# One-hots in twelve instructions with pointer scalars, and an add in four pieces, in a graph and mixture-of-experts kernel

## What is computed

```python
x = x + gnn0(layernorm(x))      # 2 graph convolutions, each a weighted sum over edges
x = x + moe0(layernorm(x))      # 6 experts, top 2 of each node
x = x + gnn1(layernorm(x))      # messages relu(mish(node)[src] + mish(edge)), summed over edges
x = x + moe1(layernorm(x))      # 8 experts, top 2

# one graph convolution of gnn0
msgs = support[edge_src] * edge_weight[:, None]
agg = jax.ops.segment_sum(msgs, edge_dst, num_segments=num_nodes)

# the message part of gnn1
y = mish(edge_features @ W_edge.T + b_edge)
msg = jax.nn.relu(x[src] + y)
agg = jax.ops.segment_sum(msg, dst, num_segments=node_features.shape[0])
```

## Time and profile before

| | |
|---|---|
| median of 3 runs | 5182.44 us |
| the profiled execution | 5180.41 us |
| its span | 5178.6 us |
| PE busy | 3895.7 us (75%) |
| POOL busy | 2875.4 us (56%) |
| DVE busy | 1965.5 us (38%) |
| ACT busy | 1566.8 us (30%) |
| mean granted TensorE clock | 0.731 |

### The profile page before, as it was taken

The page is one execution under the profiler, slowest core; times in us unless marked ns, Lnnn a source line. Parts: engine busy times, 40 slices in busy tenths (PEclk is TensorE's granted clock), DMA queues, the critical chain, the costliest instruction groups (busy, mean ns, idle before and its releaser), DMA issues. The chain is left out here.

```text
span 5178.6 us, 61257 instructions
## 1 busy us (share of the span) xinstructions
PE 3895.7 (75%) x16707; PEld 3012.1 (58%) x16707; DVE 1965.5 (38%) x4145; ACT 1566.8 (30%) x1876; POOL 2875.4 (56%) x2950
## 2 busy tenths in 40 slices
PE   3688888885788898896959966666666667769980
PEld 2455555553556565564548755666666665558870
DVE  4344344433344444433423354333333334511113
ACT  1344444443344444443201145212122123411110
POOL 0677777772777777772420055777777772600007
PEclk9778788876787778776579976555555556689995
DMA  3455555554454554552132234666666662242214
GB/s 95 140 175 171 166 173 173 177 169 116 125 156 150 157 157 150 155 156 69 66 130 85 81 113 133 197 200 197 201 199 199 200 198 61 82 154 65 65 61 144
DMA packets 336091, 733.21 MB, mean 142 GB/s; under 512 B 67797, under 2 KB 184672, under 8 KB 335897
## 3 DMA queue, kind: packets, MB, share of 16 engines
q1 hardware_dynamic: 160968, 392.16, 21.9%
q0 software_dynamic: 118176, 284.72, 20.1%
q10 hardware_dynamic: 56880, 55.58, 3.2%
HBM read 521.27 MB, written 210.91 MB: 141 GB/s over the span
## 5 line engine op out<-in xcount | busy, mean ns | idle before, releaser
L582 PE MATMUL conv_pz<-conv_we,conv_edge 128*128 128x256 f32 x3360 | 1221.0, 498 | 0.0
L1188 PE MATMUL x_pa<-x_hot,x_node 128*128 128x64 f32 x3360 | 765.7, 423 | 359.6 <-PEq L72 359.6
L464 POOL DMA_INDIRECT conv_gath<-support_table,conv_idx x840 | 808.0, 962 | 404.1 <-issue 249.8
L1173 POOL DMA_INDIRECT x_node<-node_table,x_idx x840 | 852.3, 1015 | 297.2 <-issue 234.9
L464 POOL DMA_INDIRECT conv_gath<-hidden_table,conv_idx x840 | 808.8, 963 | 346.7 <-issue 247.4
L1188 PEld LDWEIGHTS x_pa<-x_hot,x_node 128*128 128x128 f32 x3360 | 732.5, 331 | 393.0 <-issue 393.0
L582 PEld LDWEIGHTS conv_pz<-conv_we,conv_edge 128*128 128x128 f32 x3360 | 729.3, 241 | 181.7 <-issue 49.5
L573 PE MATMUL conv_ps<-conv_hot,conv_gath 128*128 128x64 f32 x3360 | 524.5, 311 | 358.9 <-DMA conv_gath<-support_table,conv_idx 187.7
L573 PEld LDWEIGHTS conv_ps<-conv_hot,conv_gath 128*128 128x128 f32 x3360 | 474.0, 221 | 404.5 <-DMA conv_gath<-support_table,conv_idx 197.3
L883 ACT ACTIVATE conv_q<-conv_q 128x1024 f32<-128x1024 f32 x210 | 221.9, 1057 | 1201.2 <-ACTq L72 1176.9
L1209 DVE TENSOR_TENSOR x_node<-x_node,x_neg 128x1024 f32<-128x1024 f32 x210 | 257.4, 1226 | 626.4 <-DMA x_node<-node_table,x_idx 626.4
(11 more groups left out here) (221 smaller groups left out, 4234.4 us busy)
## 6 DMA issues: line engine op xcount, KB each, us to landing
conv_edge<-in_edge_t SPq DMA_DIRECT2D x210, 512.0 KB, 5.0
edge_mish_table<-conv_neg SPq DMA_DIRECT2D x210, 512.0 KB, 3.1
x_neg<-edge_mish_table SPq DMA_DIRECT2D x210, 512.0 KB, 3.5
e_rows<-expert_rows SPq DMA_DIRECT2D x114, 256.0 KB, 3.0
expert_outs<-e_outs ACTq DMA_DIRECT2D x114, 256.0 KB, 2.2
expert_outs<-conv_zeros ACTq DMA_DIRECT2D x35, 512.0 KB
conv_gath<-support_table,conv_idx POOLq DMA_INDIRECT x840
conv_gath<-hidden_table,conv_idx POOLq DMA_INDIRECT x840
```

Of the source, the lines that this page charges most:

```text
L464: pool.indirect_dma_start(gath[s][:, j, :], None, table[:, :], bass.IndirectOffsetOnAxis(ap=idx[:, half, col:col + 1], axis=0),).then_inc( ...
L582: pe.matmul(ps_z[r][:, j, :], edge[r][:, m, j * P:(j + 1) * P], we[:, m, :], start=m == 0, stop=False)
L1173: pool.indirect_dma_start(node[s][:, j, :], None, c.t3[:, :], bass.IndirectOffsetOnAxis(ap=idx[:, half, col:col + 1], axis=0),).then_inc(g ...
L1188: last = pe.matmul(ps_a[n][:, m, :], node[s][:, j, m * P:(m + 1) * P], hot[n][:, j, :], start=j == 0, stop=j == CG - 1)
```

## The change

In `stage_conv`, `one_hots` first copies the half's 12 columns of `rel` and of the weights into a small tile `at_hot`, and then makes the 12 one-hots with one `tensor_scalar` each: its one tensor input is `iota` (64 columns), and its two scalars are pointers to a column of `at_hot`, compared with and multiplied by in the same instruction. In `stage_edges`, the add of `neg` to `node` is done chunk by chunk, in four instructions of 128x256; the semaphore that ScalarE waits for is raised by the last.

```diff
+        at_hot = [sb(f"at_hot{half}", [P, 2, HALF_COLS]) for half in range(2)]
...
             def one_hots(i, half):
-                part_of = lambda a: a[:, bass.ds(i * (SLOTS * CG) + half * HALF_COLS, HALF_COLS)].unsqueeze(2).to_broadcast([P, HALF_COLS, W])
-                link(dve, nc.vector.tensor_tensor(hot[half][:], c.iota[:].unsqueeze(1).to_broadcast([P, HALF_COLS, W]), part_of(rel), ALU.is_equal), own)
-                nc.vector.tensor_tensor(hot[half][:], hot[half][:], part_of(c.weight), ALU.mult).then_inc(hot_ready[half], 1)
+                part_of = lambda a: a[:, bass.ds(i * (SLOTS * CG) + half * HALF_COLS, HALF_COLS)]
+                nc.vector.tensor_copy(at_hot[half][:, 0, :], part_of(rel))
+                link(dve, nc.vector.tensor_copy(at_hot[half][:, 1, :], part_of(c.weight)), own)
+                for j in range(HALF_COLS):
+                    last = nc.vector.tensor_scalar(hot[half][:, j, :], c.iota[:], at_hot[half][:, 0, j:j + 1], at_hot[half][:, 1, j:j + 1],
+                                                   ALU.is_equal, ALU.mult)
+                last.then_inc(hot_ready[half], 1)
...
                 dve.wait_ge(gathered[s], k * (IT * CG * 16) + i * (CG * 16) + CG * 16)
-                nc.vector.tensor_tensor(node[s][:], node[s][:], neg[s % RING][:], ALU.add).then_inc(own, 1)
+                for j in range(CG):
+                    last = nc.vector.tensor_tensor(node[s][:, j, :], node[s][:, j, :], neg[s % RING][:, j, :], ALU.add)
+                last.then_inc(own, 1)
```

## The result

The changed kernel takes 5126.89 us (median of 4 runs, 5119.7 to 5141.69) against 5178.93 us of the kernel before, run in turn with it on the same chip: a ratio of 0.9903, interval 0.9881 to 0.9925. The prediction was 5141 us. The profiled execution is the slowest of the four, 5141.69 us with a span of 5139.9; against the profiled 5180.41 us of before it is 39 us shorter, not 52.

A forecast was written before the change was run, and what follows sets the result against it. POOL's gathers were taken to bound both aggregations and the edge stage. -28 - 16 + 3 = -41 us from 5180.4 gave 5139, and 5141 us for the median of runs; own range 5118 to 5163, overall 5112 to 5186.

The forecast's parts named there:

- 840 times (gather + gap): Both aggregations and edge stage: POOL never rests, so its gathers and 0.30 us gaps set each stage's length.
- Edge stage, -28 us: Edge stage: 58 us of gather excess removed, 20 and 10 us of waits returned by pieces and one-hots.
- term for the pieces: Edge stage: gathers that meet a piece of the add wait 0.095 us on average, 210 times: 20 us.
- term for the one-hots: Edge stage: the two-input one-hot instruction now comes closer before the next gather and delays some: 10 us.
- Rival 2: Edge stage: pieces don't help, saved waits return elsewhere; only the aggregations count: 5169 us, chance 0.21 with its no-change end.
- Aggregations, -16 us: Both aggregations: 31 us of gather excess removed, 15 us returned by the bursts of twelve tensor_scalar.
- rival 1: Aggregations: bursts of tensor_scalar cost POOL nothing, so -30 us there: 5127 us, chance 0.14.
- the danger: Aggregations: double-rate tensor_scalar may hold what POOL needs; 27 or 1 us by length of hold, 15 taken.
- Index waits, +3 us: Aggregations: VectorE's later adds bring the index copies nearer to POOL's need, costing 3 us.
- own sign of being wrong: POOL: index waits that add up to over 20 us would show the prediction wrong.
- Sum: Whole kernel: edge stage -28, aggregations -16 and index waits +3 make -41 us.
- Rival 3: Aggregations: POOL's second demand is many small grabs, each losing to a tensor_scalar; +56 us, 5238 us, chance 0.11.

The follow-up runs named there:

- f1: The changed kernel itself, both parts, run again against the kernel before (5184.49 us): 5138.83 us, ratio 0.9919.
- f2: The kernel before with only the edge stage's add in four pieces, against the kernel before (5184.49 us): 5155.77 us, ratio 0.9953.
- f3: The kernel before with only the aggregations' one-hots by pointer scalars, against the kernel before (5184.49 us): 5160.35 us, ratio 0.9971.
- the wide form: The changed kernel with one 128x768 tensor_scalar in place of the twelve of 128x64 in the aggregations: 6245.46 us, a single run.
- f4: The changed kernel with the edge stage's one-hots also by pointer scalars, four pieces kept: 5130.72 us, ratio 0.9899 to the kernel before.

## Why the prediction was right

- *What bounds.* "840 times (gather + gap)" held on the chips where the kernel before takes 5180 us: busy and idle time of POOL account for f1, f2 and f3. It does not hold for this kernel everywhere, which the profile of one chip could not show.
- *Edge stage, -28 us.* -34 in the first profile, -31 in f1, -35 in f2. The term for the pieces was 20: 222 gathers had a piece under way 0.13 us after their start, at a mean of 1037 ns, so 222 x 0.091 = 20. The term for the one-hots (L1204, now L1209) was 10 and came out at 77 x (993 - 946) = 4, in f1 6, of which the kernel before had 4 already. The longest wait, 1217 - 946 = 0.27, is the 0.26 of one piece. Rival 2 is excluded by f2: 0.9953, not 1.
- *Aggregations, -16 us.* The mis-sized step, with rival 1's value: 31 us of excess became 1, so -30. I took 15 as a middle between a hold of duration less 0.17 and a hold of the 64 columns alone. L503's median is 308 ns (312 was forecast) and the wide form shows the double rate and blocks gathers, so the danger was real. But the wide form holds nothing in its first 0.28 us, not 0.17, which leaves about 0.03 of the 0.31 us of a 64-column one; the 326 gathers with one under way had a mean of 948 ns.
- *Index waits, +3 us.* 20 us in the first profile, 7 in f1, 10 in f3. The size was too small, and the cause was put in the wrong place in part. The prediction had VectorE's later adds bring the copies nearer to POOL's need; in the first profile VectorE stood idle for TensorE's sum before each of the 16 longer waits, so what POOL's shorter gathers ran into was the pace of TensorE's sums, as far as the trace shows. I took the few waits of the earlier trace rows as the measure and asked neither how much nearer POOL's own gain brings its need, nor what the stretches of low clock add. The prediction's own sign of being wrong, index waits that add up to over 20 us, was met there (28.6 us in 200 to 1200 us), and the time still came out.
- *Sum.* -28 - 16 + 3 = -41 was -34 - 30 + 20 = -44 in the profiled pair, whose spans differ by 39. The terms for the aggregations and the index waits were off by 14 and 17 us in opposite directions; that they cancelled was luck. The median of the four runs, 5126.89, lies at rival 1's 5127. f1's 5138.83 lies at the forecast; the kernel before is 5.6 us slower on that chip.
- *Rival 3* (many grabs, each lost) is false for bursts of `tensor_scalar` and, but for the three gathers of f4, for pieces of 256 columns; beside eight pieces of 128 columns gathers do lose turn after turn.
- The Trainium skill (SBUF — State Buffer, "Who interferes with whom") says a `tensor_scalar` in a two-port mode contends with GpSimd's reads and writes. This case agrees for the wide form, which delays a gather at 0.13 and at 0.83 us. The twelve short instructions in a row cost the 1680 gathers about 1 us in all.

## What to carry over

Where GpSimd issues gathers without rest and VectorE shares its time, count the gathers over their median duration and see which VectorE instruction ends with each wait: that sum is the most that can be won (here 89 us, of which 64 us left the gathers and 52 the median time). Split a long two-input instruction into pieces, but measure the piece: 256 columns handed over at the next piece but for three gathers in f4, 128 did not. Try it on more than one chip: four pieces gained 0.5% on one and cost 3% on two others. And what is taken from the bounding engine shows up first as waits for the copy that feeds it; look there, and at stretches of low granted clock, before counting the whole gain.

## What the runs showed of the hardware

- The same kernel took 5184 us on one chip and 6341 and 6420 us on two others, and an edit worth -0.5% on the first cost 3% there. On the two, VectorE's long waits for TensorE's sum ended 2.0 to 2.7 us after the gathers' last packet (all 34 in the second run with pieces).
- Single-input `tensor_scalar` from SBUF with pointer scalars runs at 0.53 ns a column, and a 128x64 one lasts 308 ns; in a run of twelve one starts every 0.23 us ((2.81 - 0.31) / 11).
- A gather has two demands that VectorE can hold up, 0.13 and about 0.83 us after its start. A wide `tensor_scalar` holds up the first only if it started at least 0.15 us before the gather; otherwise the gather goes first.
- Between VectorE pieces of 128x256 with two SBUF inputs no gather waited over 0.27 us in seven of eight profiles, and three did in f4 (0.54 us at most); between pieces of 128x128 some waited for the whole burst, 1.6 us.
- Without the 840 products with the bias TensorE's mean granted clock was 0.646, the lowest of all runs on that chip, in the slowest of them; which is cause and which effect is open.
